# Attention and a 4-bit MLP on one core: other slots for score tiles, decoding and Wo, and half the value parts

## What is computed

```python
xn = _layernorm(x)
# attention: 16 heads of width 32, 4 key/value heads, causal, with an ALiBi bias
q = (xn @ Wq) ...; k, v = split(xn @ Wkv) ...
scores = einsum(q, k) / sqrt(32) + bias            # lower triangle only
out = softmax(scores) @ v ... @ Wo + bo
# mlp: three weights of 4096 x 512, each 4-bit code times a scale per 32 codes
gate = xt @ Wg.T; up = xt @ Wu.T
mlp = (gelu(gate) * up) @ Wd.T
x + out + mlp
```

## Time and profile before

| what | us |
|---|---|
| median of 3 runs (1639.86 to 1642.94) | 1640.24 |
| the profiled execution | 1641.02 |
| its span, from the first to the last instruction | 1639.2 |
| busy: PE, DVE, POOL, ACT | 1429.3, 1297.4, 1000.8, 975.9 |
| starts of two turns of the loop, 7 and 8 | 749.2, 838.9 |
| the last turn | 1470.9 to 1588.2 |

### The profile page before, as it was taken

The page is one execution under the profiler, slowest core; times in us unless marked ns, Lnnn a source line. Parts: engine busy times, 40 slices in busy tenths (PEclk is TensorE's granted clock), DMA queues, the critical chain, the costliest instruction groups (busy, mean ns, idle before and its releaser), DMA issues.

```text
span 1639.2 us, 28993 instructions
## 1 busy us (share of the span) xinstructions
PE 1429.3 (87%) x9281; PEld 684.1 (42%) x9281; DVE 1297.4 (79%) x2639; ACT 975.9 (60%) x2124; POOL 1000.8 (61%) x670
## 2 busy tenths in 40 slices
...
GB/s 219 231 176 175 171 119 170 149 161 154 160 163 144 160 155 165 145 152 149 166 158 153 157 151 160 147 174 136 173 154 154 153 158 153 147 152 133 120 155 198
DMA packets 784799, 260.97 MB, mean 159 GB/s; under 512 B 734512, under 2 KB 755896, under 8 KB 784392
## 3 DMA queue, kind: packets, MB, share of 16 engines
...
## 4 chain that ended last, share of the span: by engine, by line
DVE 30%; PE 18%; issue 14%; ACT 10%; DMA 10%; POOL 6%; SPq 4%; ACTq 0%; DVEq 0%; POOLq 0%
DMA pt<-pair 8%; PE up_ps L1348 5%; ACT p L1475 5%; POOL pair L1734 5%; DVE mxp L1588 4%; DVE acc L1545 4%; PE gate_ps L1348 4%; PE s_ps L1370 3%; DVE dec L369 3%; DVE wf L382 3%; DVE prod L1569 2%; PE down_ps L1326 2%; ACT gl L1456 2%; DVE s_ps L1590 2%; DVE dec L373 2%
## 5 line engine op out<-in xcount | busy, mean ns | idle before, releaser
L1734 POOL TENSOR_TENSOR pair<-p,pair 128x1024 f16<-128x1024 f32 (+7 forms) x384 | 615.2, 1610 | 347.3 <-ACT pair L1485 344.9
L1475 ACT ACTIVATE p<-s_ps,shift 128x512 f32<-128x512 f32 (+3 forms) x640 | 393.2, 619 | 222.6 <-DVE shift L1609 220.9
L1370 PE MATMUL s_ps<-kst,qst 128*128 128x512 f32 (+3 forms) x640 | 344.7, 540 | 115.2 <-ACT p L1475 106.9
L1485 ACT ACTIVATE pair<-p 128x1024 f16<-128x1024 f32 (+7 forms) x384 | 308.3, 808 | 100.4 <-DMA pt<-pair 97.3
L1588 DVE TENSOR_REDUCE mxp<-s_ps 128x1 f32<-128x512 f32 x384 | 260.2, 683 | 103.5 <-PE s_ps L1370 101.5
L1742 POOL TENSOR_TENSOR il<-prod,ih 128x512 f16<-128x512 f32 x128 | 156.2, 1220 | 149.7 <-DVE ih L1577 149.7
L1370 PEld LDWEIGHTS s_ps<-kst,qst 128*128 128x128 f32 x640 | 123.2, 193 | 233.6 <-ACT p L1475 157.9
L1326 PE MATMUL down_ps<-wh,ih 128*128 128x512 f16 x506 | 195.9, 387 | 28.2 <-DVE acc L1545 28.2
L1326 PE MATMUL down_ps<-wh,il 128*128 128x512 f16 x506 | 193.0, 381 | 16.0 <-POOL il L1742 16.0
L1348 PE MATMUL up_ps<-xh,wh 128*128 128x512 f16 x512 | 200.2, 391 | 0.0
L1348 PE MATMUL gate_ps<-xh,wh 128*128 128x512 f16 x512 | 197.6, 386 | 0.6 <-DVE gl L1561 0.6
...
## 6 DMA issues: line engine op xcount, KB each, us to landing
o<-oraw SPq DMA_DIRECT2D x256, 64.0 KB, 2.0
...
pt<-pair SPq DMA_TRANSPOSE x384, 4.3
...
```

Source lines behind the costliest of these rows:

```text
L1370: nc.tensor.matmul(s_ring[n % len(s_ring)][:, 0:cols], qst[:, c % 2, i4 * P:(i4 + 1) * P], kst[:, m * CH:m * CH + cols], start=True, stop= ...
L1475: nc.scalar.activation(p32[p % PR][:, at:at + cols], s_ring[n % len(s_ring)][:, 0:cols], ACT.Exp, bias=shift[t % len(shift)][:, 0:1], accu ...
L1485: nc.scalar.activation(pair[n % PH][:, 0:cols], p32[n % PR][:, 0:cols], ACT.Copy).then_inc(phi_done, 1)
L1734: nc.gpsimd.tensor_tensor(pair[n % PH][:, cols:2 * cols], p32[n % PR][:, 0:cols], pair[n % PH][:, 0:cols], ALU.subtract).then_inc(plo_done, 1)
```

## The change

- **Score tiles.** The three-block tiles 8 to 11 start in slots 4, 7, 10 and 13, so each follows the one before it directly (before: 4, 8, 11, 15). The four-block tiles 12 to 15 start in slots 16, 22, 27 and 33 (before: 18, 23, 28, 33). Between tile 12 and 13 there are now two empty slots, between 13 and 14 one, between 14 and 15 two, where there was one each. Everything that hangs on a tile (exponentials, parts, transposes, values) moves with it.
- **Decoding.** The 15 steps get slots of their own, and `rows_hi`, `rows_lo`, `turn_rows` and `load_raw` of the three weights move to slots (15, 26, 38), (16, 27, 39), (18, 29, 41) and (21, 32, 44), from (13, 23, 33), (14, 24, 34), (16, 26, 36) and (19, 29, 39).
- **Values.** `v_parts` holds only the two parts that are used; `load_v` is one DMA with 2 KB in a row for each partition. Two memsets of POOL in the preamble and SP's wait for them go.
- **First codes.** `load_raw(0, 1)` moves from the first slot of turn 0 to just before the loop.
- **Last turn.** Wo is loaded in slot 1 instead of 12; `wo_max` comes in slots 14, 16, 17, 19 (before 17 to 20); the store of its result goes alone in slot 21, the spreading in slot 28 (before both in 27); `wo_scale` in 37 (29), `wo_high` in 38, 40, 42, 43 (31 to 34), each `wo_low` a slot later; the load of x in 46 (41).

```diff
-TILE_START = tuple(range(4)) + (4, 6, 8, 10) + (12, 16, 19, 23) + (26, 31, 36, 41)
+TILE_START = tuple(range(4)) + (4, 6, 8, 10) + (12, 15, 18, 21) + (24, 30, 35, 41)
-DECODE_FROM = (8, 18, 28)
+DECODE_SLOTS = ((4, 7, 10, 13, 14), (16, 19, 22, 24, 25), (28, 31, 32, 34, 37))
-LOAD_EARLY_AT, LOAD_FULL_AT, SPREAD_TOPS_AT, LOAD_X_AT = 12, 25, 27, 41
+LOAD_EARLY_AT, LOAD_FULL_AT, STORE_TOPS_AT, SPREAD_TOPS_AT, LOAD_X_AT = 1, 25, 21, 28, 46
-WO_MAX_AT, WO_SCALE_AT, WO_HI_AT = (17, 18, 19, 20), 29, (31, 32, 33, 34)
+WO_MAX_AT, WO_SCALE_AT, WO_HI_AT = (14, 16, 17, 19), 37, (38, 40, 42, 43)
...
-                nc.gpsimd.memset(vt[:, :, :, 1, :], 1.0).then_inc(vt_filled, 1)
-                nc.gpsimd.memset(vt[:, :, :, 3, :], 0.0).then_inc(vt_filled, 1)
...
                     sp.wait_ge(values_done, i * UNITS)
-                    for part in range(2):
-                        sp.dma_start(vst[:, :, part * HD:(part + 1) * HD],
-                                     v_s[i // REP, :, :, 2 * part * HD:(2 * part + 1) * HD]).then_inc(v_in, 16)
+                    sp.dma_start(vst[:], v_s[i // REP]).then_inc(v_in, 16)
...
+                sp.wait_ge(w_in[0], 16 * W_DMAS)
+                load_raw(sp, 0, 1)
...
-                def spread_tops():
+                def store_tops():
                     sp.wait_ge(wtop_done, 1)
                     sp.dma_start(w_s.rearrange("(p o) -> p o", o=1), wtop).then_inc(wtop_out, 16)
+                def spread_tops():
                     sp.wait_ge(wtop_out, 16)
```

More of the change, by code:

```diff
@@ L136 @@
 PLAN = plan()
-DECODE_FROM = (8, 18, 28)
-DECODE_AT = {s + step: (m, step) for m, s in enumerate(DECODE_FROM) for step in range(5)}
-ROWS_HI_AT = {s + 5: m for m, s in enumerate(DECODE_FROM)}
-ROWS_LO_AT = {s + 6: m for m, s in enumerate(DECODE_FROM)}
-TURN_ROWS_AT = {s + 8: m for m, s in enumerate(DECODE_FROM)}
-LOAD_RAW_AT = {s + 11: m for m, s in enumerate(DECODE_FROM)}
+DECODE_SLOTS = ((4, 7, 10, 13, 14), (16, 19, 22, 24, 25), (28, 31, 32, 34, 37))
+DECODE_AT = {s: (m, step) for m, slots in enumerate(DECODE_SLOTS) for step, s in enumerate(slots)}
+SCALES_READY_AT = DECODE_SLOTS[0][0]
+ROWS_HI_AT = {slots[-1] + 1: m for m, slots in enumerate(DECODE_SLOTS)}
+ROWS_LO_AT = {slots[-1] + 2: m for m, slots in enumerate(DECODE_SLOTS)}
+TURN_ROWS_AT = {slots[-1] + 4: m for m, slots in enumerate(DECODE_SLOTS)}
+LOAD_RAW_AT = {slots[-1] + 7: m for m, slots in enumerate(DECODE_SLOTS)}
 LOAD_Q_AT = {46: (1, 2), 6: (0, 3), 20: (1, 0), 37: (1, 1)}
@@ L187, in build @@
     k_s = nc.dram_tensor("k_parts", [2, KVH * HD, T], F32, kind="Internal").ap()
-    v_s = nc.dram_tensor("v_parts", [KVH, P, NT, 4 * HD], F16, kind="Internal").ap()
+    v_s = nc.dram_tensor("v_parts", [KVH, P, NT, 2 * HD], F16, kind="Internal").ap()
     aug_s = nc.dram_tensor("aug_rows", [HEADS * AUG, T], F32, kind="Internal").ap()
@@ L408, in storing_steps @@
         e[n] for n in ("q_s", "k_s", "aug_s", "qst", "kst", "p_out", "q_in", "k_in", "k_last"))
-    vt = wh[1][:, 0:2].rearrange("p m a n -> p (m a n)").rearrange("p (j g a d) -> p j g a d", j=TPC, g=KVH, a=4)
+    vt = wh[1][:, 0].rearrange("p a n -> p (a n)").rearrange("p (j g a d) -> p j g a d", j=TPC, g=KVH, a=2)
     orows = acc[:, NT - 1, OROWS_AT:OROWS_AT + P]
@@ L539, in preamble @@
         vscale_done = sem("vscale_done")
-        vt_filled = sem("vt_filled")
         os_turned = sem("os_turned")
@@ L1245, in body @@
                                 load_full(sp, 0)
+                            if s == STORE_TOPS_AT:
+                                store_tops()
                             if s == SPREAD_TOPS_AT:
```

10 lines of the change are left out of this document (4 added, 6 removed).

## The result

| | before | after |
|---|---|---|
| median | 1638.89 us (1638.62 to 1642.94) | 1623.01 us (1616.81 to 1632.65) |
| ratio, with its 95% interval | | 0.9903 (0.9886 to 0.9919) |
| the profiled execution | 1641.02 | 1616.81 |
| turns 1 to 14, mean | 90.4 | 89.8 |
| the last turn | 117.3 | 99.3 |

The change makes the kernel 16 us faster. The forecast was some 98 us, so the sign was right and the size was not: 1623 lies outside the range of 1500 to 1600. The profiled execution of after is the fastest of its runs, which scatter over 16 us.

The account below looks back on a forecast made before the run. It took PE to set the time, with DVE close behind. 15 turns gave 65 us, the values 10 and the last turn 23, together 98 off, so 1542 us; range 1500 to 1600.

Parts of the forecast that it names:

- second half of a turn and `il`, less the first half's loss: Normal turn: waits of tiles 13, 15 and il go, 4.5 us gained; first half loses 0.2 more; net 4.3 a turn.
- end of a turn: Slots 38 on: added ACT, POOL and SP work set at nothing; bounds 1 us gain, 3.2 us loss.
- values: Loads of the values in turns 4, 8, 12, 3 us saved each, and 1 for the first load: 10 us.
- last turn: 117.3 to 94 us: DVE's waits go, but Wo's load stops PE 10 us at the values of tiles 4 and 5.
- turn 0: Counted among the 15 turns that each gain 4.3 us.
- the slower rival: End of a turn: rows_hi, rows_lo and two transposes in series cost 6.8 us a turn, 1644 in full; chance 0.04.
- DVE as the bound of the first half: First half: three of four direct followers wait 2.4 us each, saving falls to 1.5 a turn, 1586; chance 0.18.
- "wrong if" sentence: Forecast is wrong if a turn's first half takes over 39 us or the tiles' waits appear at its end.
- Its other sign: The first half of a turn takes over 39 us.
- the rival of the hidden steps: First half: spreading cuts the decoding loss to 1 us, a turn saves 7.9, 118 in all: 1490; chance 0.13.

Follow-up runs that it names:

- p_values: The kernel before with only one DMA for a load of the values and the first codes loaded ahead of the loop: 1626.3 us, ratio 0.9943.
- third_early: The changed kernel with the third weight's decode steps back in slots 28 to 32, and its rows_hi, rows_lo, turn_rows and load_raw moved back with them: 1586.7 us.
- steps_early: The changed kernel with only the third weight's five DVE decode steps back in slots 28 to 32; rows_hi, rows_lo, turn_rows, load_raw stay in 38, 39, 41, 44: 1639.3 us.
- rowshi_short: The changed kernel with rows_hi of the third weight working on 128 of its 1024 columns, part of the computation left out: 1614.8 us.

## Why the forecast was wrong

Against the profiled execution of before, the forecast took 98 us off and after takes 24.2 off. By parts (turns by the starts in PE's timeline):

| term | forecast | measured |
|---|---|---|
| second half of a turn and `il`, less the first half's loss | -4.3 a turn | -4.47 (slots 7 to 41) |
| end of a turn | 0 (bounds -1 and +3.2) | +3.91 in slots 42 to 6, +4.58 in slots 42, 47 and 2 alone |
| values | -10 | -9 (p_values) |
| last turn | -23 | -17.9 |
| turn 0 | -4.3, as any | +1.7 |

- **Score tiles, decoding, `il`: right in sum.** The waits of tile 13, tile 15 and `il` went: slots 20 to 41 gave 4.13 us (forecast 4.5). Slots 7 to 19 gave 0.3 where a loss of 0.2 was forecast. The first half cost less at tile 9 (0.16 us of waiting in slot 8, forecast 1.5) and as forecast at tile 12 (1.72 in slot 17, forecast some 2). A wait of 1.14 for the transposes of tiles 10 and 11 in slot 26 was not foreseen.
- **End of a turn: the step that failed.** I wrote "I set this at nothing". The rows for it were there: `rows_hi` 1.06, `rows_lo` 2.12, two transposes 3.5. I had them as the slower rival, 6.8 in series, at 0.04, and argued against it with the idle time of POOL and ACT over a turn. The averages said nothing on the 10 us in which tile 15's parts, the gelu and the next head's first parts all need these engines. The bound of 3.2 left out SP and the clock. 14 x 4.6 = 64 us of the 74 missed on the profiled execution lie here. Two runs show it from the other side: third_early, with everything of the third weight back, is 36 us faster, though `il` and slot 32 take 2.3 us a turn; and from steps_early to third_early, where the four steps alone move, it is 52.6 us.
- **Values: right.**
- **Last turn: the mechanism right, the size 5 off.** The stop is 9.82 for 10, behind Wo's load as the prediction said (the share of 0.26 fits its reason, the shape), and DVE's wait for `wo_tops` went. Not foreseen: 3.04 in slot 44, behind DVE's sum, which stands behind `wo_low` (its instruction at 1554.70 takes 2.60 us), and 2.46 for a transpose in slot 36.
- **Turn 0** has no gain: its slot 17 takes 7.44 us, with 4.07 of waiting for ACT's exponentials. But turn 0 differs by up to 5.7 us between the kernels above, and the same slot takes 3.22 in rowshi_short, so the +1.7 may be chance.
- **Rivals.** DVE as the bound of the first half (1586) did not come true. The end of the turn came at 4.6 of its 6.8 us; the forecast's own "wrong if" sentence named it. Its other sign came too, though not for its reason: slots 0 to 19 take 39.8 us in the mean (38.0 before), all of the growth and more in slot 2. In the rival of the hidden steps the sum is off: 4.5 + 4.2 - 1 is 7.7 a turn and not 7.9, which makes it 1493 and not 1490.
- The last 8 us of the miss are the profiled executions' distances to the medians, 6.2 in after and 2.1 in before. After scatters over 16 us, before over 4 beside it and over up to 12 in the later timings. What makes it scatter wasn't tried.
